# Local attention stage: masked keys released one group at a time, gate instructions ahead of the exponentials, output transposes behind the probabilities'

## What is computed

```python
lin_out = _linear_attention(h @ wq_lin + bq_lin, h @ wk_lin + bk_lin, h @ wv_lin + bv_lin)
win_out = _window_attention(h @ wq_loc + bq_loc, h @ wk_loc + bk_loc, h @ wv_loc + bv_loc, rel_bias)
gate_in = jnp.concatenate([lin_out, win_out, h], axis=-1)
gate = jax.nn.sigmoid(jnp.maximum(gate_in @ wg1 + bg1, 0.0) @ wg2 + bg2)
out = gate * lin_out + (1.0 - gate) * win_out
return out @ wo + bo + x
```

## Time and profile before

| | |
|---|---|
| median of three runs | 2846.63 us (2842.55 to 2849.23) |
| profiled execution, time | 2842.8 us |
| profiled execution, span from first to last instruction | 2840.9 us |
| busy, share of the span | PE 86%, DVE 70%, ACT 60%, POOL 41% |
| mean granted clock of TensorE | 0.944 of full speed |
| stage `at2`, from its first score product to its last instruction | 1876 to 2129 us, 8 sequences, about 30.5 us each |

### The profile page before, as it was taken

How to read it: one execution, slowest core, us unless ns; L and a number is a source line. 1 busy time by engine, 2 the same in 40 slices (tenths; PEclk the granted TensorE clock), 3 DMA queues, 4 the chain that set the end, 5 groups by cost and what they waited for, 6 DMA issues and landing times. The chain is left out here.

```text
span 2840.9 us, 37719 instructions
## 1 busy us (share of the span) xinstructions
PE 2448.3 (86%) x10998; PEld 1399.6 (49%) x10998; DVE 1979.1 (70%) x3955; ACT 1695.2 (60%) x3534; POOL 1150.7 (41%) x951
## 2 busy tenths in 40 slices
PE   7999978388898989898878899968878998799977
PEld 5766644244454444454433344445553444555555
DVE  6888755499999999999965444355644444577754
ACT  3555523398988888989943244347753443466643
POOL 1000010399999999999950000032210001254432
PEclk9999979699999999999989999989998998999998
DMA  2000033134343434344433211100002110000000
GB/s 102 1 1 1 1 109 64 60 147 153 148 155 144 153 146 152 146 152 147 164 144 76 76 60 60 60 1 1 0 1 88 77 60 27 1 1 0 0 0 16
DMA packets 34611, 205.53 MB, mean 72 GB/s; under 512 B 4000, under 2 KB 5152, under 8 KB 13216
## 3 DMA queue, kind: packets, MB, share of 16 engines
q1 hardware_dynamic: 34464, 203.83, 20.0%
HBM read 201.19 MB, written 2.62 MB: 72 GB/s over the span
## 5 line engine op out<-in xcount | busy, mean ns | idle before, releaser
L1266 POOL TENSOR_TENSOR mam_state_c<-mam_state,weights_r 128x1024 f32<-128x1024 f32 x256 | 599.5, 2360 | 67.6 <-DVE mam_state L1214 66.9
L1214 DVE TENSOR_TENSOR_SCAN mam_state<-banks,mam_dbu 128x1024 f32<-128x1024 f32 x256 | 579.8, 2275 | 5.2 <-ACT banks L1342 4.1
L1425 PE MATMUL banks<-mam_state_c,identity 128*128 128x512 f32 x1024 | 507.1, 633 | 9.9 <-POOL mam_state_c L1266 9.4
L1342 ACT ACTIVATE banks<-mam_dt,mam_a_neg 128x255 f32<-128x255 f32 x1024 | 423.8, 461 | 47.7 <-DVE mam_state L1214 45.6
L1425 PEld LDWEIGHTS banks<-mam_state_c,identity 128*128 128x128 f32 x1024 | 196.7, 202 | 230.6 <-issue 184.9
L1192 DVE TENSOR_TENSOR mam_dbu<-banks,weights_r 128x1024 f32<-128x1024 f32 x224 | 266.9, 1203 | 9.9 <-ACT banks L1350 9.9
L424 ACT ACTIVATE at_probs<-banks,at_nmax 128x256 f32<-128x256 f32 x256 | 118.0, 473 | 137.7 <-DVE at_nmax L365 137.7
L2386 POOL TENSOR_TENSOR at_attention<-at_relu 128x512 f32<-128x512 f32 x128 | 131.1, 1043 | 124.3 <-ACT at_relu L2430 82.8
L896 DVE TENSOR_TENSOR m2a_hidden<-m2a_gelu,m2a_comb_spread 128x512 f32<-128x512 f32 x120 | 80.7, 690 | 116.4 <-ACT m2a_gelu L923 113.8
L896 DVE TENSOR_TENSOR m2b_hidden<-m2b_gelu,m2b_comb_spread 128x512 f32<-128x512 f32 x120 | 80.7, 690 | 116.5 <-ACT m2b_gelu L923 114.0
L923 ACT ACTIVATE m2b_gelu<-banks,weights_r 128x512 f32<-128x512 f32 x128 | 85.2, 686 | 101.7 <-PE banks L943 101.6
(11 more groups left out here) (520 smaller groups left out, 5132.9 us busy)
## 6 DMA issues: line engine op xcount, KB each, us to landing
weights_r<-mam_bc_rows SPq DMA_DIRECT2D x128, 1024.0 KB, 4.6
m2a_comb_spread<-m2a_comb_rows SPq DMA_DIRECT2D x15, 1024.0 KB, 7.1
m2b_comb_spread<-m2b_comb_rows SPq DMA_DIRECT2D x15, 1024.0 KB, 8.3
m1a_comb_spread<-m1a_comb_rows SPq DMA_DIRECT2D x14, 512.0 KB, 7.1
m1b_comb_spread<-m1b_comb_rows SPq DMA_DIRECT2D x14, 512.0 KB, 7.2
weights_r<-in_mb SPq DMA_DIRECT2D x1, 4332.0 KB, 13.0
weights_r<-in_m SPq DMA_DIRECT2D x1, 4200.0 KB, 13.8
weights_r<-in_a SPq DMA_DIRECT2D x1, 2632.0 KB, 13.1
```

The costliest lines, as they stand in the source:

```text
L1214: dve.tensor_tensor_scan(flat2(h[:, i % 4, :, :, :]), decay(i), flat2(dbu[:, i % 4, :, :, :]), 0.0, ALU.mult, ALU.add).then_inc(h_ready, 1)
L1266: pool.tensor_tensor(hc[:, j % 4, :, :, :], h[:, j % 4, :, :, :], c_rows(j), ALU.mult).then_inc(hc_ready, 1)
L1342: i = act.activation(decay(j)[:, o + 1:o + S], dt[:, q, c, 1:S], ACT.Exp, scale=aneg[:, l, k:k + 1])
L1425: k = pe.matmul(y_bank(q)[:, :], K.ident[:, :], flat(hc[:, j % 4, n, :, :]), start=(j == 0 and n == 0), stop=(j == NP - 1 and n == 1))
```

## The change

It has three parts, all in this stage.

1. The four `km` instructions each raise `qk_ready`, and PE waits before each group's scores for that group's count only. The instruction of group 0 stays in slot 14; those of groups 1 to 3 move to the end of slot 15, behind the output copy, the exponential and the probability copy of that slot. The linear product of slot 1 waits for all four, since it overwrites what they read.
2. On ACT, the Relu of slot 8 and the Tanh of slot 10 move ahead of the exponential of the same slot.
3. On PE, the transposes of `lin` and `win` in slot 6 move behind the probability transposes of that slot (head 4).

```diff
@@ scalar, prepare(i, s, q) @@
                     if i == 14:
...
                         act.activation(qc[:, q, :], K.ps[7][:, 0:S], ACT.Identity, bias=bqs[:, :], scale=SCALE)
-                        for g in range(G):
-                            k = act.activation(km[:, q, g, :], K.ps[7][:, S:2 * S], ACT.Identity, bias=bkm[:, g:g + 1],
-                                               scale=rows_of[:, g:g + 1])
-                        k.then_inc(qk_ready, 1)
+                    if i in (14, 15):
+                        for g in ((0,), (1, 2, 3))[i - 14]:
+                            act.activation(km[:, q, g, :], K.ps[7][:, S:2 * S], ACT.Identity, bias=bkm[:, g:g + 1],
+                                           scale=rows_of[:, g:g + 1]).then_inc(qk_ready, 1)
@@ scalar, slot(i, now, last, nxt) @@
+                    if last and i == 8:
+                        act.wait_ge(g1_ps, last[0] + 1)
+                        act.activation(g1[:, :], K.ps[6][:, 0:S], ACT.Relu, bias=f("bg1")).then_inc(g1_ready, 1)
+                    if last and i == 10:
+                        act.wait_ge(g2_ps, last[0] + 1)
+                        act.activation(gate[:, :], K.ps[6][:, 0:S], ACT.Tanh, bias=bgh[:, :], scale=0.5).then_inc(gate_ready, 1)
                     if now:
                         s, q = now
                         act.wait_ge(max_ready, s * H + i + 1)
...
                         k.then_inc(exp_ready, 1)
-                    if last and i == 8:
...
-                    if last and i == 10:
...
@@ tensor, slot(i, now, last, nxt) @@
-                        if i == 0:
-                            pe.wait_ge(qk_ready, s + 1)
                         if i % 4 == 0:
+                            pe.wait_ge(qk_ready, s * G + g + 1)
                             if not (isinstance(s, int) and s == 0 and g == 0):
                                 pe.wait_ge(max_ready, s * H + 4 * g)
...
                         if i == 1:
                             pe.wait_ge(kl_ready, s + 1)
-                            pe.wait_ge(qk_ready, s + 1)
+                            pe.wait_ge(qk_ready, s * G + G)
...
-                    if last and i == 6:
...
-                        k.then_inc(lw_ps, 1)
                     if nxt:
...
                         k.then_inc(pt_ps, 1)
+                    if last and i == 6:
+                        s, q = last
+                        pe.wait_ge(win_ready, s + 1)
+                        if now:
+                            pe.wait_ge(lin_ready, now[0] + 1)
+                        for n, src in enumerate((lin[:, q, :, :], win[:, :, :])):
+                            for t in range(TS):
+                                k = pe.transpose(K.ps[7][:, n * S + t * P:n * S + (t + 1) * P], src[:, t, :], K.ident[:, :])
+                        k.then_inc(lw_ps, 1)
                     at = lagged(i, 6, H, now, last)
```

More of the change, by code:

```diff
@@ L1758, in slot @@
                         k.then_inc(exp_ready, 1)
-                    if last and i == 8:
-                        act.wait_ge(g1_ps, last[0] + 1)
-                        act.activation(g1[:, :], K.ps[6][:, 0:S], ACT.Relu, bias=f("bg1")).then_inc(g1_ready, 1)
-                    if last and i == 10:
-                        act.wait_ge(g2_ps, last[0] + 1)
-                        act.activation(gate[:, :], K.ps[6][:, 0:S], ACT.Tanh, bias=bgh[:, :], scale=0.5).then_inc(gate_ready, 1)
                     at = lagged(i, 2, H, now, last)
@@ L1836, in slot @@
                             k.then_inc(lin_ps, 1)
-                    if last and i == 6:
-                        s, q = last
-                        pe.wait_ge(win_ready, s + 1)
-                        if now:
-                            pe.wait_ge(lin_ready, now[0] + 1)
-                        for n, src in enumerate((lin[:, q, :, :], win[:, :, :])):
-                            for t in range(TS):
-                                k = pe.transpose(K.ps[7][:, n * S + t * P:n * S + (t + 1) * P], src[:, t, :], K.ident[:, :])
-                        k.then_inc(lw_ps, 1)
                     if nxt:
```

## The result

| | before | change |
|---|---|---|
| median | 2846.79 us (6 runs, 2842.55 to 2849.23) | 2826.49 us (6 runs, 2825.03 to 2833.51) |
| profiled execution, time and span | 2842.8 and 2840.9 us | 2832.5 and 2830.7 us |
| mean granted clock of it | 0.944 | 0.940 |

The change takes 0.9936 of the time before, with an interval of 0.9924 to 0.9948: 20.3 us less, against 20.0 forecast. The profiled execution of the change is one of its two longest runs, so the two profiles stand only 10.3 us apart. That difference needs explaining too.

A forecast was written before the change was run, and what follows sets the result against it. No engine is full, so a chain across engines sets the period. Gains of 9.6 + 3.5 + 7.0 = 20.1 us, called 20, take the median from 2846.6 to 2826.6 us, range 2820 to 2837.

The forecast's parts named there:

- I take 1.2 us for all eight: Masked keys by group: DVE's linear copy and group 1's scores come 1.2 us earlier at eight boundaries, 9.6 us.
- If it came to light twice: Loop's branch on PE's sequencer at the boundary, 0.213 us each: if uncovered twice it costs 0.4 us, kept as a bound.
- I take 0.5 us, 7 times: Transposes of lin and win behind head 4's in slot 6: value product starts 0.5 us earlier, seven times, 3.5 us.
- 0.35 + 0.65 = 1.0 us: Relu and Tanh moved earlier on ACT: group 1's value product gains 0.35 plus 0.65 us, seven times, 7.0 us.
- Rival 2: Slot 1's linear product, held by late keys, gives back most of the masked-key gain; 2831.6 to 2836.7 us, chance 0.09.
- Rival 1: Gate part meets another limit, head 7's probability copy or DVE's linear query; gain 13 us, 2833.5 us, chance 0.11.
- Rival 3: POOL's norm or the Tanh's way to the output product sets the period; gain under 5.7 us, 2842, chance 0.06.
- Rival 4: TensorE's clock falls to 1.2 GHz in part of the stage, up to 19 us per sequence, 2865 us; chance 0.02.

The follow-up runs named there:

- p5: The change with all four masked keys written together in slot 14, signals still by group; median 2827.26 us, ratio 0.9928 to the kernel before.
- p8: The change with one more ACT instruction, to a spare tile, ahead of slot 15's three late keys; median 2838.01 us, ratio 0.9966 to the kernel before.
- p1: The kernel before with only the masked keys signalled and placed by group; median 2835.04 us, ratio 0.9952.
- p7: The kernel before with only the Tanh moved ahead of the exponential of slot 10; median 2840.70 us, ratio 0.9976.
- p12: The change unedited, run and profiled a third time; median 2830.37 us, ratio 0.9944 to the kernel before.
- p10: p8 with two unused PE products in the wait ahead of slot 1's linear product; median 2835.15 us, ratio 0.9961 to the kernel before.
- p9: The kernel before with two unused 512-column PE products in the wait for the masked keys; median 2850.28 us, ratio 1.0012.
- p11: The change with one unused PE product in the wait ahead of slot 1's linear product; median 2824.89 us, ratio 0.9934 to the kernel before.
- p6: The kernel before with only the Relu moved ahead of the exponential of slot 8; median 2845.47 us, ratio 0.9991.

## Why the prediction was right

The sum stands at 20.1 us, the medians give 20.3, 20.4 and 16.3, and the traces, with the clock's loss in the first sequence taken out, give 231.65 - (218.49 - 3.25) = 16.4 us from first scores to last plus 1.4 ahead of them: 17.8. The forecast of a period of 27.8 us found 28.05. The range and the side were right, and so was the mechanism, one cycle through all three places. But each term was a little too large, and the nearly exact median owes something to chance.

- **"I take 1.2 us for all eight", 9.6 us.** Measured: 8.7. The start of the scores moved by 1.37 at each boundary, as worked out (1.35), and DVE's copy came to 3.42 us behind it, as worked out (2027.85 - 2024.42 = 3.43). What was off is the base, and "for all eight". The forecast read the copy's old place, 3.28, at the boundary of the earlier trace rows; there the loop jumps back, and at the four boundaries inside the loop where it does not it is 3.21. So the copy gains 1.16, and 0.02 on the way from the copy to group 1's scores and 0.06 behind them are lost too: 1.08 for each of six boundaries. The first gives 1.28, the last 0.70, where its missing norm was named and then passed over. That makes some 8.5, and the rest comes from the next point.
- **"If it came to light twice", the loop's branch, at most 0.4 us.** It came to light and cost nothing. At the two boundaries where the loop jumps back, the scores start 6.15 and 6.22 us behind group 3's instead of 5.98, 0.4 together; but the stretch behind them is shorter by the same, 6.65 and 6.60 instead of 6.82, since PE then waits for the fourth key in any case. Before, the same boundaries had a first stretch of 6.81 and 6.66 instead of 6.59, and in p5, where no late key covers it, the first jump adds 0.17 us that do not come back. So the branch cost 0.3 us before, and that is gone.
- **"I take 0.5 us, 7 times".** Measured 0.44 seven times, 3.1 us. Before, 1.03 us passed from the start of the transposes of `lin` to the value product; now 0.59 (2055.32 to 2055.91). The forecast had taken 0.53 of the 1.03 away, which leaves 0.50 for the transposes of `lin` and `win`; ahead of the value product they took 0.59. The reason for these 0.09 us is not shown. ACT's copy did not hold anything: the output copy starts 1.14 us behind the value product, 1.13 before.
- **"0.35 + 0.65 = 1.0 us".** Measured 0.26 and 0.63 apart, 0.90 together in six sequences and 0.63 in the last, 6.0 us. The Relu's term was off, since head 9's maximum was next, 0.09 us behind. The forecast had asked what is late next for the Tanh but not for the Relu.
- **Rival 2, most is given back at slot 1**: p5 and p8 measure its mechanism directly. It is real and worth 0.23 a boundary. In p1 the stretches from group 0 to group 1 grew by 1.7 us in all, 0.67 of it at the last boundary, of which the late keys are 0.2. The rival had 5 to 10.
- **Rival 1, another limit for the gates**: a wait for the Tanh of 0.54 us is left, but the gain came. **Rival 3** needed another chain right behind; the three parts adding up excludes it as far as 2.4 us a period.
- **Rival 4, the clock**: named with 0.02, with the wrong size. It falls for 3.4 us at a time, which cost the chain between nothing (p7) and 1.5 us (p5), or rises late in the first sequence, which cost 3.2. The forecast read the low clock of the earlier trace rows as lying ahead of the stage's work; the stretch of before above, 1876.0 to 1883.1 at 0.50, shows it until 6.7 us into the first sequence. It did not cost the gain in any run, but it may well make the difference between the change's two groups of runs, of which only the upper was ever profiled. The Trainium skill (TensorE: Matmul & The Clock Gate, A second HAM failure mode) says that small pauses between groups of products can let the clock swing. The traces of p8 and p12 agree, with pauses of 1.72 and 1.44 us ahead of a stretch at 0.51; the change's first profile shows 1.43 us without one, and the kernel before 1.39 to 1.50 at every boundary behind its clock's rise.

What stays open is whether the length of the pause causes these falls. That all seven falls begin at a pause speaks for it, and so, weakly, do p8 and p10; the 43 long pauses without a fall speak against it as the only cause, and p9 and p11 cannot decide. Open, too, is why two of three batches show 2.5 us more than the traces account for. The kernel before may lose such stretches too: its own profile shows none, but those of p6 and p7, whose boundary is the same, show one each. At two falls in 34 pauses and some 1.1 us a fall, an estimate from the counts above, that makes under half a us for its seven pauses, so most of the 2.5 us stay unexplained.

## What to carry to other kernels

Take the starts of one instruction that comes once per group, and tabulate the stretches between them: they are the same within 0.01 us from sequence to sequence, outside the boundaries where the loop jumps back, so an edit of 0.3 us shows there, where the median of the runs needs several us. When a wait is released early on a cycle across engines, the gain is the wait less what the deferred work now holds up; ask at each step what is late next, also for the smallest term. Split a signal by consumer first, and defer the producers only where there is other work that their engine must do.

## What the runs showed of the hardware

PE's clock can fall to half in the middle of a stage in which it is busy 89% of the time (24.95 of 27.90 us), for 3.4 us, and this adds nothing (p7) to 1.5 us (p5) to the chain. All seven such falls in fourteen profiles began at a pause of PE of 1.44 to 2.00 us, but 43 other pauses of at least 1.43 us had none; in p8 two of the boundaries with waits of 1.72 us had a fall, while the others, and one of 1.90, had none. The same kernel's first sequence ran in 25.96 or 29.21 us, by where the clock rose. At the two places where the stage's loop jumps back, PE's next products came 0.17 and 0.24 us later in the change, where no wait covers them, near the 0.213 us of the earlier trace rows; in p1 and p5 it was 0.17 at the first and nothing at the second.
